# A fused attention and channel-mix block on one core: softmax scaling moved from the probabilities to the output, more transposes through DRAM, new timetables

## The reference, cut to what matters

```
xn  = layernorm(x)
q   = xn @ Wq + bq + pe            # 8 heads of 128
k,v = xn @ Wkv + bkv ; k += pe     # one head of keys and values, shared
p   = softmax(causal(q @ k.T * 128**-0.5))
att = (p @ v) @ Wo
r   = sigmoid(mix(xn, mu_r) @ W_r.T)           # mix: with the token before
ffn = r * (relu(mix(xn, mu_k) @ W_k.T)**2 @ W_v.T)
out = x + att + ffn
```

## Time and profile before

| | |
|---|---|
| runs | 1482.39, 1481.65, 1481.39 us; median 1481.65 |
| the profiled execution | 1482.44 us, span 1480.7 us |
| TensorE clock granted | 0.998 of 2.4 GHz |
| PE busy | 1467.7 us, 99% |
| DVE busy | 1220.7 us, 82% |
| POOL busy | 1157.3 us, 78% |
| ACT busy | 1070.8 us, 72% |
| DMA | 177.53 MB, mean 120 GB/s |

### The profile page before, as it was taken

One profiled execution on the slowest core, in us unless ns is written; L12 is line 12 of the kernel. 1 busy time (PEld: TensorE's weight loads), 2 busy tenths in 40 slices (PEclk: granted clock), 3 DMA queues, 4 the chain that ended last, 5 costly groups with the idle time before them and its releaser, 6 DMA issues.

```text
span 1480.7 us, 36472 instructions
## 1 busy us (share of the span) xinstructions
PE 1467.7 (99%) x11670; PEld 1440.2 (97%) x11670; DVE 1220.7 (82%) x3376; ACT 1070.8 (72%) x2569; POOL 1157.3 (78%) x1614
## 2 busy tenths in 40 slices
PE   8999999999999999999999999999999999999998
PEld 7999999999999999999999999999999999999998
DVE  6988868988688886888868898788977889778885
ACT  5777677776677767777677776777767777777774
POOL 6778877788777887778877788777887788877785
PEclk9999999999999999999999999999999999999999
DMA  4134622346224562244622455124551245512464
GB/s 129 42 107 133 201 88 68 107 140 206 80 60 114 150 189 84 63 116 146 194 73 70 117 156 187 60 70 127 173 174 48 80 131 168 181 31 77 138 189 130
DMA packets 228972, 177.53 MB, mean 120 GB/s; under 512 B 44976, under 2 KB 224176, under 8 KB 228784
## 3 DMA queue, kind: packets, MB, share of 16 engines
q1 hardware_dynamic: 227936, 174.80, 39.9%
q10 hardware_dynamic: 848, 0.40, 0.1%
HBM read 86.51 MB, written 79.17 MB: 112 GB/s over the span
## 4 chain that ended last, share of the span: by engine, by line
PE 96%; DVE 2%; POOL 1%; issue 1%; ACT 0%; DMA 0%; SPq 0%; DVEq 0%; POOLq 0%; ACTq 0%
PE pS L1108 32%; PE pO L1255 24%; PE pG L1108 16%; PE pG L1195 10%; PE pT L1211 9%; PE pS L1195 1%; PE pO L1298 1%; PE pG L1153 0%; PE pS L1153 0%; PE pO L1263 0%; POOL X L617 0%; DVE Y L988 0%; POOL pt L584 0%; DVE pt L1008 0%; DVE X L1087 0%
## 5 line engine op out<-in xcount | busy, mean ns | idle before, releaser
L1108 PE MATMUL pS<-kt,qt 128*128 128x288 f32 (+41 forms) x2304 | 462.8, 330 | 1.4 <-POOL qt L559 1.1
L825 ACT ACTIVATE X<-X,bias 128x16 f32<-128x16 f32 (+56 forms) x512 | 375.5, 734 | 70.3 <-DVE bias L1087 67.8
L617 POOL TENSOR_SCALAR X<-X,rec 128x16 f32<-128x16 f32 (+62 forms) x504 | 362.6, 719 | 53.5 <-DVE rec L978 31.2
L1108 PEld LDWEIGHTS pS<-kt,qt 128*128 128x128 f32 x2304 | 365.0, 189 | 13.0 <-issue 1.3
L584 POOL TENSOR_TENSOR pt<-pt 128x896 fp32r<-128x896 f32 (+5 forms) x184 | 325.6, 1769 | 61.5 <-ACT pt L746 59.4
L1255 PE MATMUL pO<-pt,v 128*128 128x256 f32 x2080 | 293.5, 284 | 1.1 <-DVE ot L1066 1.0
L1087 DVE CUSTOM_DVE_ANT_1 X<-pS,mask 128x528 f32<-128x528 f32 (+31 forms) x256 | 245.5, 959 | 34.5 <-PE pS L1108 26.5
L1255 PEld LDWEIGHTS pO<-pt,v 128*128 128x128 f32 x2080 | 258.7, 189 | 2.4 <-DVE ot L1066 1.4
L818 ACT CAST ot<-pO 128x256 fp32r<-128x256 f32 x256 | 95.7, 374 | 206.3 <-PE pO L1255 116.2
L1008 DVE TENSOR_TENSOR pt<-pt,pT 128x512 fp32r<-128x512 f32 (+3 forms) x432 | 203.2, 489 | 24.7 <-ACT pt L752 20.6
L752 ACT CAST pt<-pT 128x512 fp32r<-128x512 f32 (+3 forms) x440 | 186.5, 450 | 36.5 <-PE pT L1211 34.0
(11 more groups left out here) (138 smaller groups left out, 2303.9 us busy)
## 6 DMA issues: line engine op xcount, KB each, us to landing
park_dram<-Y SPq DMA_DIRECT2D x48, 448.0 KB, 3.1
pt<-park_dram SPq DMA_DIRECT2D x192, 112.0 KB, 3.0
park_dram<-Y SPq DMA_DIRECT2D x32, 512.0 KB, 3.3
pt<-park_dram SPq DMA_DIRECT2D x128, 128.0 KB, 2.8
park_dram<-Y SPq DMA_DIRECT2D x32, 384.0 KB, 3.0
pt<-park_dram SPq DMA_DIRECT2D x128, 96.0 KB, 2.4
park_dram<-Y SPq DMA_DIRECT2D x32, 320.0 KB, 2.7
pt<-park_dram SPq DMA_DIRECT2D x128, 80.0 KB, 2.2
```

What stands on the lines that cost most here:

```text
L617: nc.gpsimd.tensor_scalar(x_row(s, 0, w), x_row(s, 0, w), rec[:, j:j + 1], sign(s), ALU.mult, ALU.mult).then_inc(normed, 1)
L825: nc.scalar.activation(x_row(s, 0, w), x_row(s, 0, w), ACT.Exp, bias=bias[:, j:j + 1], scale=-1.0, accum_out=total[:, j:j + 1]).then_inc(e ...
L1108: last = nc.tensor.matmul(out, a[i], m[j], start=start and k == 0, stop=stop and k == n - 1)
```

## The change

- **Scaling.** POOL no longer multiplies X; X keeps the unscaled exponentials, also in the packed copies, which become plain copies. The output pO is multiplied instead: DVE takes both reciprocals of a pair at once (128x2), transposes them (a 128x64 square transpose into turn_rec), SP writes 4x2x32 numbers to DRAM (`park_rec`) and reads them back spread over all 128 partitions (`spread_rec`, 128x256), and DVE writes pO times rows into rows. ACT copies the high part from there, and POOL, not DVE, makes the low part of ot. PE's next product waits for that multiplication (o_scaled), no longer for the low part (o_lo).
- **Modes.** `MODE` now has both steps turned in nine pairs of a batch instead of two, and in row 3 one pair less is turned at all: 29 turned steps a batch instead of 23. PE's transposes fall from 1224 to 896 in the run: by 2 steps each in rows 4, 5 and 7, by 1 in row 6, plus 1 in row 3.
- **Buffers.** X is 24 blocks of 128 columns (`PLACES`) instead of 10 half rows, Y three tiles instead of two, DRAM six parking places instead of four; rows has three, turn_rec two.
- **Moved.** The bias of v and the copy of the transposed v go from DVE to ACT. For 2 of 16 pieces of q a batch the low part is made by DVE from PSUM, not by POOL. The sum by DMA goes away (unused before).
- **Timetables.** All lags are new; `V_LAG` 2 instead of 3, `T_LAG` 5 instead of 6, `PV_LAG` 7 instead of 8, `LEAD` 10 instead of 11, and in rows 4 to 7 a fetch stands two turns behind its park.

```diff
-T_LAG = 6
-PV_LAG = 8
-V_LAG = 3
-F_LAG = ((5, 0), (3, 1), (4, 7), (4, 4), (4, 1), (4, 9), (5, 5), (5, 4))
+T_LAG = 5
+PV_LAG = 7
+V_LAG = 2
+F_LAG = ((4, 2), (0, -1), (3, 5), (3, 4), (4, 4), (4, 4), (4, 4), (4, 5))
...
-MODE = ('0000', '0000', '0111', '0101', '1111', '1111', '1313', '1111')
+MODE = ('0000', '0000', '0111', '0001', '1331', '1331', '3133', '3131')
+PAD_LAG = 2
+REC_LAG = 3
+O_LAG = PV_LAG + 2
+PARK_AT = 4
+FETCH_AT = 6
+ROWS = 3
...
+            def park_rec(b, pair):
+
+                g = b * (STEPS // 2) + pair
+                sp.wait_ge(rec_turned, g + 1)
+                if g >= 4:
+                    sp.wait_ge(rows_landed[g % 4], 16 * (g // 4))
+                sp.dma_start(park_d[PARKS, g % 4, 0, :].rearrange("(t q c) -> q t c", t=2, q=4),
+                             turn_rec[0:P:32, g % 2, :, :]).then_inc(rec_parked[g % 4], 16)
+
+            def spread_rec(b, pair):
+
+                g = b * (STEPS // 2) + pair
+                sp.wait_ge(rec_parked[g % 4], 16 * (g // 4 + 1))
+                if g >= ROWS:
+                    sp.wait_ge(o_lo, g - ROWS + 1)
+                sp.dma_start(rows[:, g % ROWS, :], park_d[PARKS, g % 4, 0:1, :].broadcast_to((P, 2 * P))
+                             ).then_inc(rows_landed[g % 4], 16)
...
                     fetch(b, s)
+                if it % 2 == FETCH_AT % 2 and 0 <= it - FETCH_AT < STEPS:
+                    spread_rec(b, (it - FETCH_AT) // 2)
                 if it - V_LAG in TURNED:
                     park(b, it - V_LAG)
+                if it % 2 == PARK_AT % 2 and 0 <= it - PARK_AT < STEPS:
+                    park_rec(b, (it - PARK_AT) // 2)
...
+                first = it - O_LAG
+                if 0 <= first < STEPS and first % 2 == 0:
+                    g = b * (STEPS // 2) + first // 2
+                    pool.wait_ge(o_hi, g + 1)
...
+                    nc.gpsimd.tensor_tensor(o_out[1], rows[:, g % ROWS, :].rearrange("p (t h q) -> p t h q", t=2, h=H),
+                                            o_out[0].bitcast(F), ALU.subtract).then_inc(o_lo, 1)
...
             def turn(b, it):
-                s = it - 2
-                if 0 <= s < STEPS:
-                    j = halves_of(s)[0]
+                first = it - O_LAG
+                if 0 <= first < STEPS and first % 2 == 0:
+                    pair = first // 2
+                    g = b * (STEPS // 2) + pair
+                    dve.wait_ge(rows_landed[g % 4], 16 * (g // 4 + 1))
+                    dve.wait_ge(pv_done, g + 1)
+                    nc.vector.tensor_tensor(rows[:, g % ROWS, :], pO[:, 0:2 * P], rows[:, g % ROWS, :], ALU.mult
+                                            ).then_inc(o_scaled, 1)
+                s = it - REC_LAG
+                if 0 <= s < STEPS and s % 2:
+                    g = pair_no(b, s)
                     dve.wait_ge(exp_done, b * STEPS + s + 1)
-                    nc.vector.reciprocal(rec[:, j:j + 1], total[:, j:j + 1]).then_inc(rec_ready, 1)
...
+                    nc.vector.reciprocal(rec[:, :, 0], total[:, g % 4, :]).then_inc(rec_ready, 1)
```

More of the change, by code:

```diff
@@ L43, in fillers @@
+Q_LOW = (1, 13)
 def fillers():
@@ L54, with low_on_dve, lows, blocks_of @@
 START = [("XT", 0, 0), ("KV", 0, 0), ("Q", 0, 0), ("KT", 0, 0)] + [("Q", 0, p) for p in range(1, PAIRS)]
-def halves_of(s):
-    return HALVES[s], 1 if s < SHARED else 2
+def low_on_dve(b, c, p):
+    return b is not None and 4 * (c - 1) + p in Q_LOW
+def lows(n, p, dve):
+    k = PAIRS * (n - 1) + p if n else 0
+    own = sum(1 for x in range(k) if x % (NC * PAIRS) in Q_LOW)
+    return own if dve else (k - own + PAIRS if n else p)
+def blocks_of(s):
+    return PLACES[s], s // H + 1
 def turns_of(s):
@@ L84, in used @@
     return 2 * SUB if packed(s) else 4 * SUB if doubled(s) else P
-def sign(s):
-    return -1.0 if turned(s) else 1.0
-def summed_by_dma(s):
-    return int(MODE[s // H][s % H // 2]) == 2 and s % 2 == 0
 def zeroed(s):
@@ L102, in turned_before @@
 def turned_before(s):
-    j, n = halves_of(s)
+    j, n = blocks_of(s)
     found = []
-    for half in range(j, j + n):
+    for k in range(j, j + n):
         back = 1
-        while not halves_of((s - back) % STEPS)[0] <= half < sum(halves_of((s - back) % STEPS)):
+        while not blocks_of((s - back) % STEPS)[0] <= k < sum(blocks_of((s - back) % STEPS)):
             back += 1
@@ L112, in turned_before @@
     return found
-def scaled_by_act(s):
-    return s in SCALED and not packed(s) and not doubled(s) and not turned(s)
 def width(s):
@@ L302, in build @@
         v_neg = sem("v_neg")
-        added = [sem(f"added{i}") for i in range(ADDED)]
         v_ready = sem("v_ready")
@@ L693, in kt_out @@
                 n = chunk_no(b, c)
-                act.wait_ge(kv_ready, 2 * n + 2)
+                act.wait_ge(kv_ready, n + 1)
+                if b is not None:
+                    act.wait_ge(filled["KT"], n)
+                g = g_bank("KV", c, 0)
+                nc.scalar.activation(kv[:, 1, :], g[:, CHUNK:2 * CHUNK], ACT.Identity, bias=bkv[:, 1:2]).then_inc(v_sum, 1)
                 if c == NC:
@@ L697, in kt_out, with value_out @@
                 high = kv[:, 0, :].bitcast(R) if c == NC else kt[0][:, c * CHUNK:(c + 1) * CHUNK]
[L698 removed]
+                nc.scalar.activation(high, g[:, 0:CHUNK], ACT.Copy, scale=-1.0).then_inc(kt_hi, 1)
+            def value_out(b, c):
+                n = chunk_no(b, c)
+                act.wait_ge(filled["KT"], n + 1)
+                if b is not None:
+                    act.wait_ge(v_ready, n)
+                    act.wait_ge(v_neg, n)
+                if c == NC:
+                    act.wait_ge(kt_moved, 2 * b + 1)
+                nc.scalar.copy(kv[:, 0, :], g_bank("KT", c, 0)[:, 0:CHUNK]).then_inc(v_turned, 1)
             def kt_move(b):
@@ L776, in turn @@
                         continue
-                    if kind == "Q":
+                    if kind == "Q" and not low_on_dve(b, c, p):
                         q_out(b, c, p)
@@ L874, in kv_out @@
                 g = g_bank("KV", c, 0)
-                if b is not None:
-                    dve.wait_ge(filled["KT"], n)
                 dve.wait_ge(pet_loaded, 16 * (n + 1))
```

306 lines of the change are left out of this document (151 added, 155 removed).

## The result

The changed kernel takes **1592.94 us** (median of 4 runs, 1588.5 to 1601.1); the kernel before took 1482.02 us beside it (4 runs, 1481.39 to 1482.9). The ratio is 1.0755, 95% interval 1.0735 to 1.0774: slower by 111 us, where I had forecast 30 us faster. The profiled execution took 1588.5 us, its span 1586.8.

The account below looks back on a forecast made before the run. PE, busy for 99% of the span, was taken to bound the kernel. 1482.44 us less 32.2 for transposes plus 2.4 for lateness gave 1452.6, with the runs' median 0.8 lower 1452 us; range 1442 to 1472.

Parts of the forecast that it names:

- Transposes off PE: On PE: 328 transposes fewer over eight batches save 32.2 us, the one term on the path.
- SP's queue: Rows 4 to 7: 177 issues at 0.51 us take 90 us of 103.0, 88%, with ends of 76 and 104.
- 2.4 us of lateness: Some fetches in rows 4 to 6 come late: 0.3 us a batch, 2.4 us over the run.
- rival A: SP saturates in rows 4 to 7 from 0.58 us an issue; at 0.62 the run takes 1504 us; chance 0.11.
- the 24.0 us of waits which I let go: SP in rows 4 to 7: its 24.0 us waiting for parks to land go, since fetches stand two turns later.
- 0.78 each in a dense place: SP's issue price in the densest place, read from eight issues in 6.22 us; the quiet price was 0.43.
- Together nothing, with 1 us to either side: PE's waits at pO and Wo: the next product's shorter wait and Wo's longer one cancel, with 1 us either way.
- A tile has one turn less ... so the slack is about the same: From scores to product a turn goes, but the removed scaling was such a step, so slack is about the same.
- DVE's new wait: DVE's multiplication waits for spread reciprocals: 7 us of DMAs fit in five turns, with 1 us to spare in row 1.
- DVE's small additions: L1000, now 48 instead of 32, meeting POOL on SBUF: 27 us of DVE at worst, nothing on PE.
- DMA load: From 177.53 to 254 MB, share in rows 4 to 7 from 0.52 to 0.80, priced at nothing by itself.
- Start: First batch's time without PE work and its lower clock spell stay: nothing, plus or minus 4 us.

Follow-up runs that it names:

- fewer_transposes: Kernel before with 336 of PE's 1224 transposes left out, parts of some pT stale: 1453.17 us.
- no_spread: Changed kernel without the two reciprocal DMAs a pair; DVE copies pO unscaled into rows, so the output is not divided by the sums: 1517.03 us.
- both_reliefs: Changed kernel with one DMA a fetch and without the two reciprocal DMAs a pair (blocks in wrong order, output unscaled): 1497.19 us.
- one_fetch: Changed kernel with each turned tile read back in one DMA of 128 partitions instead of four of 32, blocks in wrong order: 1503.08 us.
- half_fetch: Changed kernel with the same DMAs, but each fetch piece brings only half its columns: 1571.56 us.
- mult_earlier: both_reliefs with DVE's instruction at pO at the end of the turn in which PE finished the pair, ahead of the mask: 1483.47 us.
- mult_earlier_whole: Complete changed kernel with DVE's multiplication of pO at the end of the turn in which PE finished the pair, ahead of the mask: 1577.74 us.
- turn_less: Kernel before, complete with its old fillers, but one turn less from a tile's scores to its transposes and product with v: 1739.71 us.
- before_more: Kernel before with two unused DMAs a pair added on SP, 142 issues in rows 4 to 7 instead of 110: 1495.08 us.
- old_table: both_reliefs with the three timetables of the kernel before (fillers, Wo, preparations of a chunk): 1608.46 us.
- one_more_pair: Kernel before with both tiles of one more pair, the third of row 7, turned by DMA: 1504.41 us, ratio 1.0152.
- fetch_turn_earlier: mult_earlier with the fetches of rows 4 to 7 one turn earlier (row 7's second tiles two turns earlier): 1679.4 us.

## Why the prediction was wrong

**Transposes off PE** (32.2 us): right in mechanism; 28.6 us in size by fewer_transposes.

**SP's queue, priced at nothing but 2.4 us of lateness: the step that failed.** I took 177 issues at 0.51 us, 90 us of 103.0; measured were 170 in the window at 0.59, 100.2 us, inside my ends of 76 and 104. SP was so 88% taken up, the share that I had forecast, and never saturated in the sense of rival A. Even so SP costs 94 to 96 us, while A had 22 at 0.62. The error was not in the duration but in the rule: I asked whether the sum of issues fits in the stretch. What the runs show is that it need not overflow. Each tile comes when its issue gets its turn in the queue, and every engine behind it works in a fixed order, as the timeline of turn 53 shows. That SP's part falls to a fifth with 32 issues fewer (no_spread against both_reliefs), and that two unused DMAs a pair cost the kernel before 12.6 us, show the same. That the 24.0 us of waits which I let go were the slack that took up such delays is my reading; no run tests it alone.

One reading of rows was wrong as well. The eight issues in 6.22 us, which I took for 0.78 each in a dense place, hold a wait of 1.6 us: the second fetch stood there until its own park had landed at 1434.0. The issues themselves took 0.55 each (one of them 1.35). So the row was no evidence for 0.78 under load, and what it did show was one DMA that waits at the head of the queue with the others behind it.

By the Trainium skill (DMA: Bandwidth & Descriptors, "Issuing engines are not separate DMA queues") the sequencer's time is usually small beside the transfer. For one DMA this case agrees: 0.50 us of issue, 2.9 us to the landing of a fetch piece of 112 KB. For the sum it does not help: one_fetch moves the same bytes with 75 issues fewer in rows 4 to 7 and gains 90 us, half_fetch moves half of the fetched bytes and gains 21.

**"Together nothing, with 1 us to either side"**, for the waits at pO and Wo: the move in mult_earlier and mult_earlier_whole gave 14 and 15 us, a term of 2 us a batch. I had read the one instance at the end of the run and counted the instructions in the chain. I had not asked what stands ahead of the new DVE instruction (the mask of the turn before), nor that Wo now waits for it too.

**"A tile has one turn less ... so the slack is about the same"**: neither shown nor refuted. turn_less loses 258 us, but with fillers that do not fit. What remains of the miss when both terms above are repaired, 1483.5 - 1452 = 31 us less 3 for the transposes, lies for the most part in row 6: 3.2 of the 4.3 us that mult_earlier still loses a batch by the prices of before, 1.7 of them in turn 51, where PE waits for a low part of POOL's. Whether it is the lost turn, the added tiles or the fillers between POOL's low parts stays open.

**DVE's new wait** for the spread rows: right, 3.8 us in 5 times. **DVE's small additions** (L1000 before): right, 566 ns in the mean for 598, 48 times. **DMA load**: the share in rows 4 to 7 was 0.74 for the 0.80 forecast; parks land in 3.9 us for 3.1, and half_fetch puts 21 us on 46 of the 254 MB, so nothing was too little. **Start**: right, the first scores come at 23.2 us for 23.4, with the same low spell; the clock cost more than thought all through the run, behind the waits. **Rivals**: A named the resource, the place and the signs, at 0.11, with a price four times too small and with a limit (0.58 us for each of 177 issues, 103.0 us) that SP's 100.2 us did not reach.

The pieces: 1452 forecast + 95 SP (as defined at mult_earlier_whole) + 14 pO + 3 transposes + 28 open = 1592. The last is what is left over, not a measurement.

## What to carry to other kernels

A queue that issues in order can cost long before its busy time reaches the stretch: price it by how late each item comes. In this case it was taken up for 61% of rows 4 to 7 in the kernel before, for 76% in before_more, which lost 12.6 us, and for 88% in the changed kernel, which lost some 95. When several engines follow fixed orders with lags counted in turns, a lag, a table of fillers or one misplaced small instruction can cost more than the work that is saved, and each is fitted to the others (turn_less, old_table, one_more_pair); find out what stands ahead of it on its engine, at the shortest turns above all. Test the gain alone (leave the work out) and the cost alone (add the issues) on the old kernel first: those two runs would have shown 29 us to win and a queue that costs 12.6 us at 76%. When a merged row of a timeline gives a time for several issues, look whether a wait lies inside before you divide.

## What the runs showed of the hardware

What an issue of SP costs does not grow with what it carries: in the changed kernel 0.56 us in the median for 1 KB (turn_rec) and 0.54 for a park of 448 KB, 0.38 for a spread row and for a park of 512 KB. A fetch of 448 KB costs 2.0 us of issues in four pieces and 0.6 in one. A single quarter lands in 2.9 us and the whole in 4.5 (mult_earlier) to 4.8 (one_fetch), but from the first issue to the last landing the four quarters take 4.9, so the split brings the tile no sooner.

After short waits scattered over a batch PE's granted clock fell to 1.2 GHz for 3.4 us at a time: ten times in the changed kernel from the second batch on, never there in the kernel before. In fetch_turn_earlier there were some thirty such spells, eight of them twice as long, and the mean clock is 0.960.
